# Sums and products moved between TensorE, VectorE and GpSimd in a Mamba layer with experts

## The reference

```python
delta = jax.nn.softplus(dt @ dt_w.T + dt_b)
A = -jnp.exp(A_log)
def step(h, inp):
    d_t, B_t, C_t, u_t = inp
    dA = jnp.exp(d_t[..., None] * A)
    h = h * dA + (d_t * u_t)[..., None] * B_t[:, None, :]
    y = jnp.einsum('bdn,bn->bd', h, C_t)
    return (h, y)
y = scan(step) + xi * Dp
y = y * jax.nn.silu(z)
return y @ out_w.T
...
x = x + mamba_both_ways(xn) + experts(xn)
```

## Time and profile before

| | |
|---|---|
| median of 3 runs | 910.14 us |
| lowest, highest run | 907.42, 910.88 us |
| profiled execution, its own time | 907.48 us |
| its span, first to last instruction | 905.7 us |
| mean granted TensorE clock | 0.891 of full speed |

### The profile page before, as it was taken

The page is one execution under the profiler, slowest core; times in us unless marked ns, Lnnn a source line. Parts: engine busy times, 40 slices in busy tenths (PEclk is TensorE's granted clock), DMA queues, the critical chain, the costliest instruction groups (busy, mean ns, idle before and its releaser), DMA issues.

```text
span 905.7 us, 10749 instructions
## 1 busy us (share of the span) xinstructions
PE 738.3 (82%) x3033; PEld 329.6 (36%) x3033; DVE 883.4 (98%) x635; ACT 696.3 (77%) x1185; POOL 802.3 (89%) x453
## 2 busy tenths in 40 slices
PE   8889867886588988989797987989878879679376
PEld 5334312331134534444343533445333432224032
DVE  6999999999899999999999999999999999999997
ACT  5998864845479889988989989897979976575650
POOL 0788787999999999898899998999798999999996
PEclk8969797687799989999899999989989897988689
DMA  8894344134355555545455626455553444462400
GB/s 234 226 278 113 116 105 142 52 101 113 114 146 169 146 190 145 166 125 139 146 144 180 174 81 208 120 171 140 175 143 91 143 97 148 113 184 61 108 0 13
DMA packets 90988, 123.60 MB, mean 136 GB/s; under 512 B 7977, under 2 KB 63274, under 8 KB 86962
## 3 DMA queue, kind: packets, MB, share of 16 engines
q1 hardware_dynamic: 88882, 118.72, 46.5%
q0 software_dynamic: 2048, 4.20, 1.5%
HBM read 75.57 MB, written 14.29 MB: 99 GB/s over the span
## 4 chain that ended last, share of the span: by engine, by line
issue 39%; POOL 30%; PE 13%; ACT 9%; DVE 6%; DMA 1%; SPq 0%; ACTq 0%; POOLq 0%; DVEq 0%
POOL hs L1485 19%; POOL sorted_tokens L1496 4%; ACT dA L1032 3%; POOL gu_w L1458 3%; DVE hs L1245 2%; PE in_b L626 2%; DVE in_b L1226 2%; PE y L660 2%; ACT L1041 2%; POOL tmpA L1418 2%; PE front L579 2%; PE front L619 2%; POOL du L1423 1%; DVE hs L1243 1%; POOL yg L1468 1%
## 5 line engine op out<-in xcount | busy, mean ns | idle before, releaser
L1485 POOL TENSOR_TENSOR hs<-hs,C_rep 128x1024 f32<-128x1024 f32 x250 | 585.4, 2362 | 45.8 <-DVE hs L1245 24.6
L1032 ACT ACTIVATE dA<-delta_rep,A_sb 128x511 f32<-128x511 f32 x512 | 335.3, 717 | 20.4 <-DMA delta_rep<-tmpA 16.3
L1226 DVE TENSOR_TENSOR in_b<-in_b,B_rep 128x1024 f32<-128x1024 f32 x256 | 301.2, 1225 | 3.3 <-PE in_b L626 2.1
L1245 DVE TENSOR_TENSOR_SCAN hs<-dA,in_b 128x1024 f32<-128x1024 f32 x128 | 286.0, 2276 | 5.4 <-PE y L660 5.1
L1243 DVE TENSOR_TENSOR_SCAN hs<-dA,in_b 128x1024 f32<-128x1024 f32 x128 | 285.6, 2274 | 0.9 <-PE y L660 0.9
L626 PE MATMUL in_b<-du,cst 128*128 128x512 f32 x256 | 162.4, 721 | 60.9 <-DVE hs L1245 43.7
L660 PE MATMUL y<-hs,cst 128*32 128x512 f32 x1016 | 136.4, 655 | 22.1 <-POOL hs L1485 22.1
L579 PE MATMUL front<-xpad,w_in 128*128 128x512 f32 x248 | 117.4, 608 | 7.2 <-ACT xi L961 5.6
L1041 ACT ACT_TABLE_LOAD x71 | 91.1, 1283 | 11.6 <-PE moe L809 7.1
L626 PEld LDWEIGHTS in_b<-du,cst 128*128 128x128 f32 x256 | 47.7, 216 | 134.4 <-issue 129.9
L579 PEld LDWEIGHTS front<-xpad,w_in 128*128 128x128 f32 x248 | 46.2, 195 | 63.2 <-issue 49.8
(11 more groups left out here) (166 smaller groups left out, 810.7 us busy)
## 6 DMA issues: line engine op xcount, KB each, us to landing
delta_rep<-tmpA SPq DMA_DIRECT2D x126, 256.0 KB, 3.9
C_rep<-dbc_scratch SPq DMA_DIRECT2D x16, 1024.0 KB, 7.3
B_rep<-dbc_scratch SPq DMA_DIRECT2D x15, 1024.0 KB, 5.2
gu_w<-in_gate_up SPq DMA_DIRECT2D x39, 384.0 KB, 3.8
dn_w<-in_down SPq DMA_DIRECT2D x39, 192.0 KB, 2.6
xs<-sorted_tokens SPq DMA_DIRECT2D x39, 64.0 KB, 3.9
sorted_ffn<-ys SPq DMA_DIRECT2D x39, 64.0 KB, 2.4
sorted_tokens<-up_f SPq DMA_DIRECT2D x9, 256.0 KB, 4.5
```

The lines of the kernel that those rows point to most:

```text
L1032: i = e.activation(dA[:, m % NA, r * L + 1:(r + 1) * L], src, ACT.Exp, scale=A_sb[:, d, 2 * p + jj, RH * rh + r:RH * rh + r + 1])
L1226: e.tensor_tensor(to, in_b[:, 2 + 2 * odd, :].unsqueeze(1).broadcast_to([P, RH, L]), by, ALU.mult).then_inc(dve_mult, 1)
L1245: e.tensor_tensor_scan(to[:, ::-1], a[:, 1:n + 1][:, ::-1], b[:, ::-1], 0.0, ALU.mult, ALU.add).then_inc(dve_scan, 1)
L1485: e.tensor_tensor(hs[:, m % NH, :], hs[:, m % NH, :], C_rep[:, u % 2, RH * rh:RH * rh + RH, :].rearrange("p r t -> p (r t)"), ALU.mult).th ...
```

## The change

Eight softplus sums (both halves of units 3, 4, 14 and 15) leave POOL. PE adds them with two identity matmuls into M (`sum_delta`, at the steps in `SUM_STEP`), and ACT copies M to `tmpA` one step later (`keep_delta`). For unit 3 DVE makes du from M (`first_du`, at the steps in `DU_STEP`); POOL still makes du of the others. The gates of halves 27 and 28 go from POOL and ACT to DVE. The products with C of steps 41, 56, 180, 217 and 226 go from DVE to POOL. The first delta loads of units 3 and 15 stand later in SP's program. The name in the code, D*u, is delta times u.

```diff
 SILU_SET, EXP_SET = "silu_and_others", "natural_log_exp_and_others"
-GATE_ON_DVE = (3, 4, 5, 2 * UNITS - 1)
-C_ON_DVE = (41, 56, 180, 217, 226, LAST - 1)
+GATE_ON_DVE = (3, 4, 5, 27, 28, 2 * UNITS - 1)
+C_ON_DVE = (LAST - 1,)
+DU_STEP = {(3, 0): 42, (3, 1): 44}
+SUM_STEP = {(3, 0): 41, (3, 1): 43, (4, 0): 57, (4, 1): 59,
+            (UNITS - 2, 0): 218, (UNITS - 2, 1): 219, (UNITS - 1, 0): 232, (UNITS - 1, 1): 235}
...
+def sums_on_pe(v, h):
+    return sum(k <= (v, h) for k in SUM_STEP)
+def du_on_dve(v, h):
+    return 1 + sum(k <= (v, h) for k in DU_STEP)
+def du_on_pool(v, h):
+    return 2 * v + h + 1 - du_on_dve(v, h)
+def sums_on_pool(v, h):
+    return 2 * v + h - sums_on_pe(v, h)
...
         act_dbc, act_dt, act_abs = sem("act_dbc"), sem("act_dt"), sem("act_abs")
+        pe_delta, act_delta = sem("pe_delta"), sem("act_delta")
         act_root1, act_base = sem("act_root1"), sem("act_base")
...
                 e.wait_ge(dve_delta, 1)
+            elif (v, h) in SUM_STEP:
+                e.wait_ge(act_delta, sums_on_pe(v, h))
             else:
-                e.wait_ge(pool_delta, 2 * v + h)
+                e.wait_ge(pool_delta, sums_on_pool(v, h))
...
         def wait_du(e, v, h):
-            if v == 0 and h == 0:
-                e.wait_ge(dve_du, 1)
+            if v == 0 and h == 0 or (v, h) in DU_STEP:
+                e.wait_ge(dve_du, du_on_dve(v, h))
             else:
-                e.wait_ge(pool_du, 2 * v + h)
+                e.wait_ge(pool_du, du_on_pool(v, h))
...
                 for v in fronts(m, -5, -8):
-                    load_pair(v, 0)
+                    if (v, 0) not in SUM_STEP or v % 2 == 0:
+                        load_pair(v, 0)
+                for v in fronts(m, -5, -5):
+                    if (v, 0) in SUM_STEP and v % 2:
+                        load_pair(v, 0)
                 for v in fronts(m, -3, -4):
...
+            def sum_delta(v, h):
+                e.wait_ge(act_log, 2 * v + h + 1)
+                if (v, h) == (3, 0):
+                    e.wait_ge(dve_route, N_POS)
+                elif (v, h) == (UNITS - 2, 0):
+                    e.wait_ge(act_fin, 2)
+                elif v == UNITS - 1:
+                    e.wait_ge(act_fin, 4 + h)
+                if sums_on_pe(v, h) > 1:
+                    e.wait_ge(act_delta, sums_on_pe(v, h) - 1)
+                if 1 < sums_on_pe(v, h) <= 1 + len(DU_STEP):
+                    e.wait_ge(dve_du, sums_on_pe(v, h))
+                e.matmul(M[:, :], ident, tmpA[:, h, :], start=True, stop=False)
+                e.matmul(M[:, :], ident, tmpB[:, h, :], start=False, stop=True).then_inc(pe_delta, 1)
...
                     e.wait_ge(act_up, NTILE)
+                if b == 2:
+                    e.wait_ge(act_delta, sums_on_pe(UNITS - 2, 1))
+                if b >= 4:
+                    e.wait_ge(act_delta, sums_on_pe(UNITS - 1, b - 4))
                 e.wait_ge(in_attn[b % 2], 16 * (b // 2 + 1))
...
                         in_proj(v, 1, 1)
+                for v, h in SUM_STEP:
+                    if SUM_STEP[v, h] == m:
+                        sum_delta(v, h)
                 for n in tiles_at(m, 8):
...
                     e.wait_ge(dve_route, N_TILE_EXPERT)
+                    e.wait_ge(act_delta, sums_on_pe(4, 1))
                     e.wait_ge(in_xs[0], 16)
...
+            def keep_delta(v, h):
+                e.wait_ge(pe_delta, sums_on_pe(v, h))
+                e.copy(tmpA[:, h, :], M[:, :]).then_inc(act_delta, 1)
...
             for m in range(STEPS):
+                for v, h in SUM_STEP:
+                    if SUM_STEP[v, h] + 1 == m:
+                        keep_delta(v, h)
                 for v in fronts(m, -14, -14):
...
+            def first_du(v, h):
+                wait_delta(e, v, h)
+                e.wait_ge(act_xi, 2 * v + h + 1)
+                e.wait_ge(pe_du, J * (v - 1 - h) + 4 + 4 * h)
+                e.tensor_tensor(du[:, du_slot(v, h), :], M[:, :], xi[:, v % 2, h, :], ALU.mult).then_inc(dve_du, 1)
...
                         gate(i)
+                for v, h in DU_STEP:
+                    if DU_STEP[v, h] == m:
+                        first_du(v, h)
                 if m == LAST + 5:
...
             def delta_du(v, h):
-                e.wait_ge(act_log, 2 * v + h + 1)
-                e.tensor_tensor(tmpA[:, h, :], tmpA[:, h, :], tmpB[:, h, :], ALU.add).then_inc(pool_delta, 1)
+                if (v, h) not in SUM_STEP:
+                    e.wait_ge(act_log, 2 * v + h + 1)
+                    e.tensor_tensor(tmpA[:, h, :], tmpA[:, h, :], tmpB[:, h, :], ALU.add).then_inc(pool_delta, 1)
                 wait_delta(e, v, h)
...
                     for v in fronts(m, (-7, -4)[h], (-8, -6)[h]):
-                        delta_du(v, h)
+                        if (v, h) not in DU_STEP:
+                            delta_du(v, h)
                 if m < LAST and m not in C_ON_DVE:
...
                     e.wait_ge(dve_scan, m + 1)

```

## The result

The median after is 901.9 us (4 runs, 897.98 to 901.95), of before on the same chip 910.5 (907.42 to 913.84); the ratio is 0.9895, with a 95% interval of 0.9859 to 0.9931. The forecast was 902.5 us within 898 to 908.5, and faster with a chance of 0.72. The profiled execution took 901.9 us with a span of 900.1, against 907.48 and 905.7 before.

The account below looks back on a forecast made before the run. DVE, busy 883.4 of 905.7 us, was taken as the bound, with POOL setting the end of two stretches. Terms -4.4 - 1.1 - 1.5 = -7.0 us from about 909.5 gave 902.5, range 898 to 908.5.

Parts of the forecast that it names:

- Stretch A: Steps 33 to 61: POOL's queue sets the end, 4.4 us gained, some 1.5 us of DVE's wait stay.
- The quicker DMAs: Steps 33 to 52: without two DVE products that slow its indirect DMAs, POOL gets 1.7 us back.
- unit 3's new chain: Steps 39 to 44: PE's sums, ACT's copies and DVE's du fit without making DVE wait, if PE is not late.
- Step 180: DVE's product with C goes to POOL, which stood idle 4.10 us there: 1.1 us gained.
- Stretch B: Steps 208 to 252: 1.5 us gained, with PE as third party; bounds from -4.8 to +1.3.
- the spread behind the cold y sum no longer costs 0.86: Near step 245: DVE's 0.86 us wait for a spread of du, at 864.55 in before, goes.
- The scan of step 238: It comes 1.4 us later than before: PE's chain 0.8 later, gate 28 ahead of it 0.6 more.
- The y sum's wait at step 245: DVE's wait of 2.04 us goes, as POOL's y sum is there by 857.5.
- All of PE's added work hides: Rival: PE's new sums cost nothing, -10.3 us in all, 899 us; chance 0.13.
- PE's chain is the new bound in full: Rival, steps 232 to 238: +1.3 us there, -4.2 in all, 905.3 us; chance 0.27 shared with unit 3's sums holding DVE.
- Slower: Rival: PE's eight sums are cold, 3.5 us each, and delay DVE; 916 us at 1.7 lost each; chance 0.08.
- The indirect DMAs don't get quicker: Rival: their length has another cause than DVE's products; -2.7 us in steps 33 to 61, 904 us; chance 0.07.

Follow-up runs that it names:

- second executions: The unchanged kernels after and before, each executed and profiled once more: 899.2 and 907.7 us.
- du on POOL: Kernel after, but unit 3's du is made by POOL again, its sum still on PE: 902.75 us, ratio 0.9925 to before.
- Bias later: Kernel after, with the last batch's bias and residual two steps later (246, not 244), behind the spread in PE's queue: 899.61 us, ratio 0.989 to before.
- PE warmed: Kernel after, plus four PE matmuls with results thrown away, two each at steps 242 and 243: 901.33 us, ratio 0.9907 to before.
- the final sums moved: Kernel after with the later bias, and the final sums of steps 221 and 237 behind the y sums on PE: 900.37 us, ratio 0.9891 to before.
- extra products in SBUF: Kernel after, plus six unused 128x1024 products on DVE while POOL issues the sort's DMAs, both operands in SBUF: 918.5 us, one execution.
- the extra ones: Kernel after, plus six unused 128x1024 products on DVE while POOL issues the sort's DMAs, first operand in PSUM: 905.7 us, one execution.
- A alone: Kernel before with only the edits of units 3 and 4 and the products of steps 41 and 56 on POOL: 904.67 us, ratio 0.9942.
- B alone: Kernel before with only units 14 and 15's sums on PE, gates 27 and 28 on DVE, products 217 and 226 on POOL: 906.82 us, ratio 0.9964.
- the last sum on POOL: Kernel after, with unit 15's second sum on POOL again: 902.34 us, ratio 0.9918 to before; with the later bias too, 899.59 us, 0.9888.

## Why the prediction was right, and where it was not

The forecast of 902.5 us is 0.6 above the median. Part of that is luck: it started from 909.5 for before, 1.0 below the median on this chip, and its gain of 7.0 is 1.6 below the 8.6 of the medians. Its parts did not all hold either.

**Stretch A, -4.4: right, in size and in cause.** Measured -4.39, -4.40 between the second executions and -4.37 alone; some 1.5 us of the wait were to stay, 1.7 did. That POOL's queue is the bound is shown by du on POOL (+2.35 against 2 x 1.27). POOL's product of step 54 ended 4.4 us sooner against step 32, as forecast. The quicker DMAs were put at 1.7 us and came to 1.5. The cover of unit 3's new chain held: PE's first sum ended at 169.9 where 169.6 was forecast, and neither du made DVE wait.

**Step 180, -1.1: right,** -1.12 in every kernel that has it.

**Stretch B, -1.5: the size is near what most profiles show (-1.6 to -1.7), though not the first (-0.3), but by luck: the working behind it was wrong in two steps that offset each other.**

- The step that failed is "the spread behind the cold y sum no longer costs 0.86". It costs 2.8 us in one profile of after (2.29 + 0.52), 1.7 in the other and in two more kernels with this queue. The working took only the y sum as slow. In PE's queue a bias and a residual stand between it and the spread, and they ran at the low clock too, 2 x 2.07 where 1.12 each is the usual. Bias later and PE warmed show both halves of that.
- The scan of step 238 was to be 1.4 us later than before. Counted from step 208's product it came 0.2 earlier (104.7 against 104.9). PE's chain, which was put 0.8 later, began 1.3 earlier (87.9 against 89.2), since gate 27 left ACT's way: the copy of z waited 0.15 us where it had waited 1.51. It reached the y sums 0.8 earlier, with unit 15's second sum in it. That the sum added so little to the chain, 14.24 us to the y sums against 13.69, is the clock: in before PE had waited 1.98 us ahead of the chain and 0.68 in after, and the residual and the output matmuls took 1.91 and 2.64 us in before, 1.02 and 1.95 in after (819.14, 820.00). PE's timeline of the kernel before:

```profile
823.69 1.91 PE L711 MATMUL front<-x_in,cst 128*128 128x512 f32 x2
825.39 2.64 PE L736 MATMUL front<-w_out,yg 128*128 128x128 f32 x16
```

- That this sum costs its time in full at step 238 was right: without it the stretch is 1.5 to 1.8 us shorter.
- The y sum's wait at step 245, put as gone, is gone. The gathers' indirect DMAs, put 0.9 us quicker, were 0.95 us quicker in all (31.62 and 30.67 us).

**Rivals.** "All of PE's added work hides" is wrong in both profiles of after. The kernel with the later bias comes to 899.6 beside that rival's 899, but still waits 1.7 us at step 238. "PE's chain is the new bound in full" is wrong for the whole kernel, though half of it is seen at step 238; unit 3's sums held nothing. "Slower" is wrong, though its price of 3.5 us for a cold sum is about right: in after two of the eight took 3.4 us (at 174.5 and 806.0), and DVE waited for neither. One of the eight was shown to cost time, 1.5 to 1.8 us at a high clock; it was slow in two kernels, the one with the final sums moved and the one with extra products in SBUF.

"The indirect DMAs don't get quicker" is refuted by the six stretched DMAs of one kernel and the none of the other. The Trainium skill ("SBUF — State Buffer", Who interferes with whom) infers that a VectorE product of two SBUF operands does not hold up the descriptors of an indirect DMA; in the runs the instruction of the indirect DMA is held, 1.81 us against 1.01 in six of six cases. Whether that is its writing of descriptors or its reading of the positions `pos_u` from SBUF no run separates, but the rival that followed from the inference is wrong. The Trainium skill's fixed surcharge for a PSUM operand ("VectorE: DVE Perf Modes", the TRN2 errata section) isn't seen: the 128x512 du of unit 3, with one operand in PSUM, takes 0.67 us, and the kernel before's 128x512 sum on DVE with both in SBUF 0.69 (at 19.97); the 128x1024 products take 1.22 us with an operand in PSUM (the extra ones) and 1.22 with both in SBUF.

**The signs.** DVE's wait near 240 is 1.72 us, within the 1 to 2 that were given, and DVE never waited for M's copies. DVE's busy time fell by 5.1 us, not 2.3; the prediction's own terms for DVE (-2.9, -1.1 and -1.0) give 5.0, so the 2.3 was a slip. "None above 1.1 us" holds for the sort's DMAs but for one, which takes 1.19 us in before (at 148.12) as in after (at 148.86). The waits near step 238 are 1.7 us, not 2 to 3. One of them, 0.49 us for the spread, is among the signs of being wrong that were given (PE late): the PE part of stretch B is where the working failed.

**The total.** By the two pairs of profiles the kernel gains 5.6 and 8.4 us, by the medians 8.6, by the ratio 0.0105 x 910 = 9.6; forecast was 7.0. The parts add up, as far as their intervals allow: by their ratios A alone gives 5.3 (3.3 to 7.3), B alone 3.3 (0.4 to 6.2), and step 180 by its row 1.1, together 9.7. Stretch by stretch the two profiles of after account for 5.8 and 7.2 us of it: -4.4, -1.1, and -0.3 or -1.7 (B alone reached -3.5 by its clock). In the profiles the rest lies in the stretches 0 to 32 and 64 to 176, where executions of all kernels differ by up to 6 us in DVE's waits for PE. Whether the change moves that part on average isn't settled.

**A faster version.** The later bias, with or without the last sum on POOL, gives 899.6 us, ratios 0.989 and 0.9888. In the profile it removes 3.0 us of waiting against the first profile of after and 1.8 against the second (26.47, 29.49 and 28.29). By the medians it gains 2.3, by the ratios, which allow for the chip, only 0.5, and the intervals overlap with that of the kernel after. So the times alone don't show that it is faster than the kernel after.

## What to carry to other kernels

In a kernel where one engine is busy 98% of the span, find for each stretch the engine that ends it, and price an edit in that engine's queue: here 2.5 us of POOL's work were worth 2.35 us in a stretch where DVE got less to do. When a wait that hid behind another is to go, read everything in the releasing engine's queue up to what is wanted next, and price it at the clock that engine will then have. If two profiles of one program differ by as much as the gain sought, compare between named instructions, stretch by stretch, and take a second profile.

## What the runs showed of the hardware

- A 128x1024 product on DVE with both operands in SBUF, run beside POOL's product of the same kind, ended 1.09 us after POOL's in six of six cases: 1.8 to 3.7 us instead of 1.22. The indirect DMA that POOL issued behind its product took 1.81 us instead of 1.01. With one operand of DVE's product in PSUM neither happened.
- PE's granted clock at the same place of the program differs between executions, and with it DVE's waits for PE, although PE is busy only 82% of the span: 112 steps in which no kernel differs took 370.9 us at a mean of 0.96 and 376.9 us at 0.93.
- A sum of two tiles on PE, 128x512 in float32, takes 1.9 us at the upper level of the clock (168.03 to the end of the second pair at 169.91) and 3.3 where the clock was low for most of it (819.04 to 822.33).
